# Values of a later cross attention made between two earlier attentions and kept in DRAM

## The reference, cut to what matters

```
v = (memory_tokens @ wv.T).reshape(B, M, NH, HD)      # memory_tokens is the context: an input
attn = softmax(where(mask, q k^T * scale, -inf))      # 16 heads of 16
out = einsum('bhlm,bmhd->blhd', attn, v) @ wo.T
return sigmoid(x @ wg.T) * out                        # x = rmsnorm(hidden_states)
```

## Time and profile before

| | us |
|---|---|
| median of 3 runs (lowest, highest) | 1206.72 (1205.46, 1207.45) |
| span of the profiled execution, first to last instruction | 1198.9 |
| PE busy | 1095.9 |
| DVE busy | 780.9 |
| ACT busy | 588.6 |
| POOL busy | 461.3 |

### The profile page before, as it was taken

The page is one execution under the profiler, slowest core; times in us unless marked ns, Lnnn a source line. Parts: engine busy times, 40 slices in busy tenths (PEclk is TensorE's granted clock), DMA queues, the critical chain, the costliest instruction groups (busy, mean ns, idle before and its releaser), DMA issues.

```text
span 1198.9 us, 20821 instructions
## 1 busy us (share of the span) xinstructions
PE 1095.9 (91%) x7384; PEld 655.3 (55%) x7384; DVE 780.9 (65%) x1500; ACT 588.6 (49%) x1212; POOL 461.3 (38%) x756
## 2 busy tenths in 40 slices
PE   5999869999988598999879999899999999999997
PEld 3666635555553154777433455577786334545455
DVE  5999877888873412333666678676888465564655
ACT  2776617878767312333366555376874432121210
POOL 6999734666644163333225345451121000000001
PEclk7999969999989799999989999999999999999999
DMA  6965345666652122553504000010000000000000
GB/s 225 322 200 172 102 113 139 157 155 160 162 118 55 27 91 82 156 162 105 171 0 140 1 1 11 27 36 2 2 2 28 1 0 1 9 9 9 10 9 27
DMA packets 75354, 95.90 MB, mean 80 GB/s; under 512 B 12883, under 2 KB 62189, under 8 KB 74573
## 3 DMA queue, kind: packets, MB, share of 16 engines
q1 hardware_dynamic: 70835, 84.92, 25.3%
q0 software_dynamic: 3408, 9.34, 2.2%
q10 hardware_dynamic: 1010, 0.31, 0.1%
HBM read 57.47 MB, written 31.27 MB: 74 GB/s over the span
## 4 chain that ended last, share of the span: by engine, by line
PE 49%; ACT 5%; DVE 4%; DMA 4%; issue 3%; POOL 2%; POOLq 0%; SPq 0%; DVEq 0%; ACTq 0%
PE cps_h L2972 6%; PE cps_h L2141 4%; PE cps_h L1604 4%; DMA xrows<-c_xr,c_place_int 4%; PE cps_o L1623 3%; PE cps_h L2991 3%; PE cps_x L3005 2%; PE cps_x L3030 1%; PE cps_o L3030 1%; PE cps_t L2991 1%; PE cps_h L2603 1%; PE cps_o L2991 1%; PE cps_t L3005 1%; PE cps_x L2541 1%; PE cps_h L2586 1%
## 5 line engine op out<-in xcount | busy, mean ns | idle before, releaser
L902 DVE TENSOR_REDUCE b_nm<-a_s 128x4 f32<-128x1024 f32 x64 | 78.2, 1222 | 36.5 <-PE a_s L982 35.4
L2734 POOL TENSOR_SCALAR f_rstd<-f_mv 128x1 f32<-128x1 f32 x16 | 3.8, 240 | 252.9 <-DVE f_mv L2886 252.8
L937 ACT ACTIVATE a_late<-a_qkv 128x512 f32<-128x512 f32 x128 | 76.3, 596 | 45.0 <-PE a_qkv L1012 44.2
L2831 DVE TENSOR_TENSOR f_prod<-f_sg,f_kept 128x512 f32<-128x512 f32 (+1 forms) x48 | 33.2, 692 | 94.8 <-ACT f_kept L2762 90.8
L2972 PE MATMUL cps_h<-residT,w_f_w 128*128 128x512 f32 x176 | 80.8, 598 | 3.4 <-DVE f_inner L2868 1.9
L937 ACT ACTIVATE a_late<-a_y 128x512 f32<-128x512 f32 x128 | 76.4, 597 | 5.0 <-PE a_y L1012 3.4
L902 DVE TENSOR_REDUCE b_nm<-a_pt 128x4 f32<-128x1024 f32 x64 | 76.8, 1199 | 0.1
L2756 ACT ACTIVATE f_sg<-cps_h 128x512 f32<-128x512 f32 (+1 forms) x24 | 14.3, 596 | 123.6 <-PE cps_h L2991 107.6
L1027 PE MATMUL a_o<-a_late,b_vt 128*32 128x256 f32 x1024 | 70.1, 393 | 0.0
L1342 POOL DMA_INDIRECT routed<-c_out,c_target x39 | 37.5, 962 | 68.5 <-ACT c_out L1423 68.2
L2012 DVE SCALAR_TENSOR_TENSOR d_acc<-d_pad,d_cw,d_acc 128x512 f32<-128x512 f32 x72 | 58.4, 815 | 6.6 <-ACT d_acc L1913 4.9
(11 more groups left out here) (434 smaller groups left out, 2887.0 us busy)
## 6 DMA issues: line engine op xcount, KB each, us to landing
kparts<-a_rest SPq DMA_DIRECT2D x48, 192.0 KB, 3.4
a_rest<-a_rest SPq DMA_DIRECT2D x64, 128.0 KB, 3.1
xrows<-in_c_fill SPq DMA_DIRECT2D x13, 387.0 KB, 4.5
c_xrow<-xrows SPq DMA_DIRECT2D x39, 129.0 KB
c_back<-routed SPq DMA_DIRECT2D x16, 256.0 KB, 3.5
a_front<-kparts SPq DMA_DIRECT2D x12, 288.0 KB
a_front<-qparts SPq DMA_DIRECT2D x36, 96.0 KB
qparts<-b_xp SPq DMA_DIRECT2D x48, 64.0 KB, 2.5
```

The lines of the kernel that those rows point to most:

```text
L902: dve.tensor_reduce(nm[s % 2][:, 4 * n:4 * n + 4].rearrange("p (g h) -> p g h", h=2), s1[step % 2][:], AX.X, ALU.max, negate=True).then_in ...
L937: act.activation(pr[g % 8][:], s2[g % 2][:], ACT.Exp, scale=SCALE).then_inc(s2_out, 1)
```

## The change

The values leave slot s of the later cross attention. A new function values_natural(t) makes them for all 128 rows of tile t at once, with two products of 128 weight columns, between the two attentions of layer 0; ACT copies them out and writes them to DRAM (rows_taken); SP reads them back in layer 1 (values_in) and POOL puts them in place (values_placed). wv is loaded at slot 12 of the self attention instead of with the later weights.

```diff
+    k.values_rows = nc.dram_tensor("values_rows", (2, T, TILES, 2, P), F32, kind="Internal").ap()
+    ROWS_BETWEEN = 9
+    values_ps = [(qkv_bank[:] if t % 2 == 0 else tr[:].rearrange("p a b -> p (a b)") if t < ROWS_BETWEEN else y_bank[:])[:, 0:D]
+                 for t in range(TILES)]
+    ROWS_AHEAD = [(TILES + (n + 1) // 2, (n + 1) % 2) for n in range(ROWS_BETWEEN)]
+    ROWS_STEP = {AHEAD + n: len(ROWS_AHEAD) + n for n in range(TILES - len(ROWS_AHEAD))}
...
+    def rows_taken(act, t):
+        act.wait_ge(rows_full, t + 1)
...
+        act.activation(staged[t], values_ps[t], ACT.Copy).then_inc(rows_out, 1)
+        act.wait_ge(rows_out, t + 1)
+        act.dma_start(k.values_rows[:, :, t].rearrange("b s h c -> (b s) (h c)"), staged[t]).then_inc(rows_kept, 16)
...
         def exps(x, g):
+            if x == 0 and g == 0:
+                act.wait_ge(rows_kept, 16 * TILES)
...
+    def values_natural(pe, t):
...
+        elif t >= 2:
+            pe.wait_ge(rows_out, t - 1)
+        if t == ROWS_BETWEEN:
+            pe.wait_ge(free.y_out, TILES)
+        for kd in range(KD):
+            ins = pe.matmul(values_ps[t], k.ctxT[:, kd, t * P:(t + 1) * P], wv[:, kd, :], start=(kd == 0), stop=(kd == KD - 1))
+        ins.then_inc(rows_full, 1)
...
         if (s, place) in PE_AHEAD:
             first_pass(pe, PE_AHEAD.index((s, place)))
+        if (s, place) in ROWS_AHEAD:
+            values_natural(pe, ROWS_AHEAD.index((s, place)))
...
             if live(s) and step >= AHEAD:
                 first_pass(pe, step)
+            if step in ROWS_STEP:
+                values_natural(pe, ROWS_STEP[step])
...
+        def values_in(sp, t):
+            if t >= RING:
+                sp.wait_ge(vbd_in, 2 * (t - RING + 1))
+            for h2 in range(2):
+                sp.dma_start(rows[t % RING][h2 * T:(h2 + 1) * T, :, :], k.values_rows[:, :, t, h2, :].rearrange("b s c -> s b c")
+                             ).then_inc(rows_in[t % RING], 16)
...
+            def values_placed(t):
+                gp.wait_ge(rows_in[t % RING], 32 * (t // RING + 1))
...
+                for h2 in range(2):
+                    half = slice(h2 * T, (h2 + 1) * T)
+                    gp.tensor_copy(vbd[t % 4][half, :, :, h2, 0:HD], rows[t % RING][half, :, :].rearrange("p b (q d) -> p b q d", d=HD)
+                                   ).then_inc(vbd_in, 1)
...
             if live(s + 1):
                 row_factor(s + 1)
+            if live(s):
+                values_placed(s)
...
-                for h2 in range(2):
-                    rows = slice(h2 * T, (h2 + 1) * T)
-                    act.activation(vbd[t % 4][rows, :, :, h2, 0:HD], values[rows], ACT.Copy).then_inc(vg_out, 1)
...
-                for b in range(2):
-                    for h2 in range(2):
-                        for kd in range(KD):
-                            pe.matmul(vg_ps[h2 * T:(h2 + 1) * T, 0, b * P:(b + 1) * P], k.ctxT[:, kd, t * P + b * T:t * P + (b + 1) * T],
-                                      wv[:, kd, h2 * P:(h2 + 1) * P], start=(kd == 0), stop=(kd == KD - 1))
```

More of the change, by code:

```diff
@@ L382, in gpsimd, with scalar @@
             between(gp, s)
-    def scalar(act):
+    def scalar(act, between):
         for dst, src in consts:
@@ L448, in scalar @@
                 exps(s - 2)
+            between(act, s)
     def vector(dve, between):
@@ L721, in cross_attention @@
     trb = tr[:, 0, :].bitcast(BF16)[:, 0:P]
+    values_ps = [(qkv_bank[:] if t % 2 == 0 else tr[:].rearrange("p a b -> p (a b)") if t < ROWS_BETWEEN else y_bank[:])[:, 0:D]
+                 for t in range(TILES)]
+    staged = [free.rest[:, n * D:(n + 1) * D] for n in range(3)] + [free.front[:, G * D:]] \
+        + [free.middle[:, G * D + n * D:G * D + (n + 1) * D] for n in range(2)] + [free.late[:, n * D:(n + 1) * D] for n in range(TILES - 6)]
+    rows_full, rows_out, rows_kept = sem("b_rows_full"), sem("b_rows_out"), sem("b_rows_kept")
     const, vt_set, gp_steps = sem("b_const_in"), sem("b_vt_set"), sem("b_gp_steps")
@@ L775, in sync_between @@
     def sync_between(sp, s):
[L776 removed]
+        if s == TILES - 4:
+            sp.dma_start(wv[:], io["e_wv"]).then_inc(const, 16)
             sp.dma_start(gamma[:], io["b_gamma"]).then_inc(const, 16)
@@ L960, in scalar @@
                     products_out(y, half)
+            if step in ROWS_STEP:
+                rows_taken(act, ROWS_STEP[step])
             x, j = divmod(step - LAG, STEPS)
@@ L1087, in _ @@
             def _(act):
-                first.scalar(act)
+                first.scalar(act, between.scalar)
                 second.scalar(act)
@@ L2276, in later_weights @@
     w = {}
-    shapes = [(f"e_{n}", [P, KD, D], F32) for n in ("wq", "wv", "wo", "wg")]
+    shapes = [(f"e_{n}", [P, KD, D], F32) for n in ("wq", "wo", "wg")]
+    w["e_rows"] = [k.sb(f"w_e_rows{v}", [P, 2, P], F32, ctx) for v in range(2)]
     shapes += [("e_nw", [P, KD], F32), ("e_mask", [P, TILES, T], mybir.dt.uint8)]
@@ L2340, in keys_in @@
             sp.dma_start(kT[c][:], k.keysT[:, :, c * CHUNK:(c + 1) * CHUNK]).then_inc(k_in[c], 16)
-        def sync(sp, s, place):
-            for c in (0, 1) if s < 0 else (2, 3):
-                keys_in(sp, c)
+        def values_in(sp, t):
[4 more added lines that the diff above has]
+                             ).then_inc(rows_in[t % RING], 16)
+        def sync(sp, s, place):
+            if s < 0:
+                keys_in(sp, 0)
+                keys_in(sp, 1)
+                sp.wait_ge(rest.y_out, TILES)
+                for t in range(RING):
+                    values_in(sp, t)
+                return
+            keys_in(sp, 2)
+            keys_in(sp, 3)
+            for t in range(RING, TILES):
+                values_in(sp, t)
         def gpsimd(gp, s, place):
@@ L2429, in values_gate_out @@
                     act.wait_ge(o_out, t - 5)
-                act.activation(gate[t % 6][:], vg_ps[:, 1, :], ACT.Tanh, scale=fac[:, t:t + 1]).then_inc(vg_out, 1)
+                act.activation(gate[t % 6][:], gate_ps, ACT.Tanh, scale=fac[:, t:t + 1]).then_inc(gate_out, 1)
             if s < 0:
@@ L2629, in tensor @@
                 if live(s):
-                    values_gate(s)
+                    gates(s)
                 if live(s - 3):
```

91 lines of the change are left out of this document (57 added, 34 removed).

## The result

| | before | changed |
|---|---|---|
| median of 7 runs on one chip, us | 1204.26 (1196.99 to 1207.45) | 1191.76 (1189.46 to 1196.49) |
| ratio of the times | | 0.9926, 95% interval 0.9896 to 0.9955 |
| profiled execution: span, us | 1198.9 | 1188.1 |
| span of a second profiled execution of each (e8, e11), us | 1205.0 | 1187.9 |

The change made the kernel 0.74% faster in this comparison, 12.5 us by the medians and 8.9 by the ratio. Compared again at the end of the experiments (e11), the ratio was 0.9851 (0.9815 to 0.9888). The two intervals do not meet, so a comparison can be further off than its own interval says, and ratios of experiments that were compared at different times have to be read with that in mind. The profiled run of the changed kernel took 1189.92 us, 1.8 us more than its span; in all seven it is 1.8 or 1.9.

What follows compares the result with a forecast made beforehand. PE was taken to bound layer 1's cross attention, DVE close behind, and no single engine the stretch between layer 0's attentions. 1198.9 - 12.9 + 4.7 = 1190.7 us of span, plus 7.8, written as 1198.3; likeliest range 1195 to 1202.

Steps and rivals of the forecast that it cites:

- the likeliest case: Whole kernel: the forecast itself, 1198.3 us, layer 1 gaining 12.9 and the stretch between attentions losing 4.7; chance 0.45.
- the three faster ones together: Whole kernel: the forecast, rival 1 and rival 4 together, 1191 to 1202.5 us with their spread; chance 0.83.
- The walk through one slot: Layer 1's cross attention: following one slot's durations without the value group gives a period of about 6.75 us instead of 7.69.
- I charge DVE 0.2 us a slot: Layer 1: POOL's copies slow DVE's addition of r and resid, making the period 6.95 us or a little under.
- the 2.8: Layer 1, slots 0 to 3, beside the state space block's end: a gain of 0.7 us each.
- Rival 3: Layer 1: both POOL copies block DVE in each slot, 0.8 us instead of 0.2, giving 1205.2 us; chance 0.09.
- The walk: Between layer 0's attentions: delays followed step by step from weights(15) to the first exponential, at about 178 instead of 173.34.
- the two candidates: End of the stretch between attentions: maxima landing at 177 to 178, or the last values' store at 177.5 to 178.
- a later 173.34 moves everything behind it by as much: Layer 0's cross attention: its steady loop of 128 steps passes on a late first exponential in full, 4.7 us lost.
- Rival 1: Between attentions: value groups fill PE's waits, the clock stays up and 4.1 us come back, 1194.2 us; chance 0.20.
- Rival 2: Between attentions: the clock falls near 160 with value groups still to come, exponential 16.2 us late, 1210.0 us; chance 0.08.
- Rival 4: Both parts: DVE loses nothing to POOL and transfers collide little, a gain of 12.5 us, 1194.2 us; chance 0.18.

Runs made afterwards that it cites:

- e8: The kernel before, unchanged, run again for its profile and spread; ratio to before 0.9998 (0.9968 to 1.0027).
- e11: The changed kernel, unchanged, compared again with the kernel before on one chip; 1188.70 us against 1204.40, ratio 0.9851.
- e4: The changed kernel with each of POOL's copies in layer 1 cut to 64x16 values, waits and order kept; ratio to before 0.9901.
- e1: Layer 0 part alone: values made and stored as in the changed kernel, layer 1 as before; 1203.59 us against 1202.09, ratio 1.0012.
- e2: Layer 1 part alone: layer 0 as before, layer 1 as changed but reading the context's own array as rows; ratio to before 0.9889.
- e3: Layer 0 part alone without the 16 transfers storing the values and without the wait for them; ratio to before 0.9984.
- e5: The changed kernel with ACT waiting later for the stores: tiles 0 to 11 before the first exponential, 12 to 15 before the fourth; ratio to before 0.9865.
- e9: The changed kernel with PE running nine and five matmuls that nothing reads during its waits before second passes; ratio to before 0.9878.
- e7: The changed kernel with the last of POOL's three casts of a context tile in the self attention done by ACT; ratio to before 0.9900.

## Why the prediction was right, and where it was off

The direction and the mechanism were right, and both parts came out better than forecast: 8.4 us forecast (8.2 by the terms of the sum); by parts it is 15.5 - 2.4 = 13.1, and the two comparisons gave 8.9 and 17.9. That the first comparison stands so near the forecast is luck: the forecast had layer 1 too small by 2.6 us and the cost between the attentions too large by 2.3. The measured median, 1191.76, lies under the 1195 to 1202 of the likeliest case and just inside the 1191 to 1202.5 of the three faster ones together.

**Layer 1: 12.9 forecast, 15.5 measured.** In the same two profiles, slots 5 to 15 gave 10.65 (the softmax of tiles 4 and 15 start 84.35 us apart before, 73.70 now), not 8.2; slots 0 to 4 gave 4.9, with slot 0's group, and the forecast was 4.7. The walk through one slot came to 6.75 us and the slot is 6.72. So the term that was mis-sized is "I charge DVE 0.2 us a slot" for POOL's copies: DVE's addition lost 0.10, and e4 shows that the slot lost nothing. The 10.65 against 8.2 is 2.4 of the 2.6 us by which layer 1 gained more than forecast. In slots 0 to 3 the 2.8 was 3.7, in slot 4 the 1.9 was 1.2. A clock below 1.00 near slot 4 is in both of these profiles; e8 and e11, without it, differ by 14.5 in column C, 15.6 with slot 0's group.

**Rival 3** is refuted by the same rows. POOL's pair took 0.95 us and lengthened DVE's addition by 0.10, not by a copy's length. The two copies one by one:
```profile
845.08 0.40 POOL L2445 COPY e_vbd<-w_e_rows 64x256 f32<-64x256 f32 x1 [0.22 <-POOL e_fac L2423]
845.53 0.49 POOL L2445 COPY e_vbd<-w_e_rows 64x256 f32<-64x256 f32 x1
```
The Trainium skill (SBUF — State Buffer, section SBUF: two separate sides) has the loser block until the other's whole instruction is over. At this place the trace shows less than that: the first copy had 0.25 us to go when the addition started, and the addition lost 0.10. In the self attention, below, it is 0.3 and 0.4 us.

**Between the attentions: 4.7 forecast, about 2.4 measured.** Column A gives 169.7 against 167.4 in the rhythm of 7.80 (two profiles each), and 173.1 against 170.5 in that of 8.16 (three and one). Single profiles of an unchanged layer 0 are 2.7 us apart (166.0 and 168.7), so the 2.4 is an estimate from few samples; e1's time, 1.4 us and at most 5, agrees with it. e11 ran in the rhythm of before and 0.1 us ahead of it, so its steps can be laid beside the earlier trace rows. Timeline of e11:
```profile
146.81 1.04 PE L617 MATMUL a_pt<-ident,a_late 128*128 128x128 f32 x8
...
155.98 1.09 PE L642 MATMUL a_o<-a_rest 128*128 128x256 f32 x4
...
157.31 0.42 DVE L511 TENSOR_TENSOR a_rest<-a_o,resid 128x256 f32<-128x256 f32 x1 [0.40 <-PE a_o L645]
...
163.20 1.21 DVE L913 TENSOR_REDUCE b_nm<-a_pt 128x4 f32<-128x1024 f32 x1
...
167.65 0.22 PE L1051 MATMUL a_tr<-identb,b_mp 128*96 128x128 bf16 x1
...
168.95 0.78 SPq L800 DMA_DIRECT2D a_front<-b_mt  x1
...
172.13 0.33 ACTq L953 DMA_DIRECT2D values_rows<-a_late  x1
...
175.84 0.38 PE L1062 MATMUL a_qkv<-a_front 75*128 75x256 bf16 x2 [3.73 <-DMA a_front<-b_mt]
...
178.81 0.60 ACT L967 ACTIVATE a_late<-a_qkv 128x512 f32<-128x512 f32 x1 [6.71 <-DMA values_rows<-a_late]
```

| step | before | e11 | late by (with the 0.1) | forecast |
|---|---|---|---|---|
| weights(15) | 146.18 | 146.81 | 0.7 | 0.8 |
| output(15) | 153.43 | 155.98 | 2.7 | 2.7 |
| sums(15) | 155.56 | 157.31 | 1.9 | 1.9 |
| step 7's maxima | 161.51 | 163.20 | 1.8 | 2.3 |
| turn_maxima(0) | 164.82 | 167.65 | 2.9 | 4.2 |
| SP's issue | 166.69 | 168.95 | 2.4 | 3.8 |
| first second pass | 172.72 | 175.84 | 3.2 | 4.3 to 5.3 |
| first exponential | 173.34 | 178.81 | 5.6 | 4.7 |
| first reciprocal | 200.18 | 203.79 | 3.7 | 4.7 |

The walk held up to the sums of tile 15. Behind them a step took 1.31 us, not 1.4, and the clock stayed at 1.00 while before's steps ran at 0.50. The maxima's transfer took 6.9 us from SP's issue to PE's start, inside the 6.5 to 7.5 that I gave it. A collision is not seen in it: the same step took 5.8 to 7.9 us in the seven profiles with stores and without filling, and 5.8 to 7.0 in the four without stores (before, e8, e2, e3). What ended ACT's wait were the values' stores, as one of the two candidates was: 5.6 us late. The last store landed 6.7 us after its issue at 172.13, where I had 3 to 4, but the last value group was done at 171.7 and not at 173.5. So that the first exponential stands near my 178 is in part luck.

The step that failed is "a later 173.34 moves everything behind it by as much": 1.9 of the 5.6 us came back before the first reciprocal. Two things in the traces give time back. PE's first second pass was only 3.2 us late, and PE worked ahead while ACT waited. And behind the first exponential PE stood at half speed for 10.4 us in before and for 7.7 in e11, by the granted clock of windows of 0.5 us. From the first exponential to the first reciprocal it is 26.8 us in before, 25.0 in e11, 28.0 in e5 (13.7 us at half speed) and 22.2 in e9 (none). How much of the 1.9 belongs to which is not shown.

Rival 1 was half right. The values' matmuls kept the clock of e11 up until the wait for the transfers, and its clock fell after all, as the forecast had it (1.00 in 160 to 175, below in 175 to 185), but for 10.2 us, where both profiles of before had 23.9 and e2 37.5. e9 prices the remaining fall at about 2.5 us (A 170.8 against 173.2).

**Rival 2** did not come: groups of 1.03 us and first passes left PE next to no gap up to 169. **Rival 4** came nearest: 12.5 us, where the parts give 13.1, and DVE's part of the reason is shown. That the transfers collide little fits the maxima's landing; what the stores did was to hold ACT, and e1 against e3 puts that at 3.4 us with an uncertainty of about 5.

## What to carry to other kernels

Work put into a stretch where an engine idles can pay for part of its place by keeping the clock at its upper level; ask of a filled gap and of a removed wait alike what the clock does behind it. A wait that ends before a stretch at half speed is worth taking away only together with the low clock: by single profiles the later wait alone gave nothing to the first reciprocal, the fill alone 2.5 us, both 4.3 to 4.6. And where executions fall into different rhythms, compare stages and not spans: column C moved by 1.9 us between executions with the same layer 1, the span of before by 6.1.

## What the runs showed of the hardware that I had not expected

The self attention has two steady rhythms, 7.80 and 8.16 us from one of DVE's maxima to the next, constant to 0.02 us from the sixth tile to the fourteenth, and the same program takes either. Timeline of the changed kernel, rhythm 8.16:
```profile
115.49 0.95 POOL L359 TENSOR_TENSOR a_front<-a_front,a_rest 128x256 f32<-128x256 f32 x1
115.82 0.89 DVE L492 TENSOR_TENSOR a_front<-a_front,a_sc 128x256 f32<-128x256 f32 x1
...
117.03 0.84 DVE L471 TENSOR_SCALAR resid<-a_rest,a_mv,a_rstd 128x256 f32<-128x256 f32 x1
117.05 0.67 POOL L363 TENSOR_TENSOR a_front<-a_front,a_rest 128x256 f32<-128x256 f32 x1
...
118.80 1.19 DVE L456 TENSOR_REDUCE a_mx<-a_s 128x16 f32<-128x1024 f32 x1
```
The same program (e11), rhythm 7.80:
```profile
118.92 0.62 DVE L492 TENSOR_TENSOR a_front<-a_front,a_sc 128x256 f32<-128x256 f32 x1
...
119.34 0.73 POOL L359 TENSOR_TENSOR a_front<-a_front,a_rest 128x256 f32<-128x256 f32 x1
119.86 0.40 DVE L471 TENSOR_SCALAR resid<-a_rest,a_mv,a_rstd 128x256 f32<-128x256 f32 x1
...
121.50 1.23 DVE L456 TENSOR_REDUCE a_mx<-a_s 128x16 f32<-128x1024 f32 x1 [0.23 <-PE a_s L606]
```
In the fast one DVE waits for PE's scores. In the slow one DVE meets POOL's subtractions, and the two instructions shown take 0.27 and 0.44 us longer. The wait tables of 60 to 130 list no wait of DVE in the slow one, while in the fast one it waits 2.2 us for PE's scores. That nothing then brings the two apart again is my reading; no run tests it, and e7, which took work off POOL, did not bring the fast rhythm. It costs 4.2 us over the self attention (117.3 against 113.1 from its first to its last copy of turned weights, in the two profiles of before). What decides between them I don't know. The first difference that the traces show is the third distance of two maxima, 8.23 to 8.25 us ahead of the fast rhythm and 8.29 or more ahead of the slow one, in all 13 profiles that took one of the two. The granted clock of the first 30 us does not part them: it is 0.50 from 15 to 20 in one of each (before and e1) and 1.00 up to 30 in others of each (e3 and the changed kernel).
